# A decoder layer on one core: sums over keys and gate product in column groups of TensorE, with normalisations moved from VectorE to ScalarE and GpSimd

## The reference

```python
x = layernorm(x + attention(x))          # rotary q and k, attention between the heads of one token
x = layernorm(x + xattn(x, ctx, ctx))    # an mLSTM cell: q = x, k = v = ctx
x = layernorm(x + ffn(x))                # 8 low-rank experts, one chosen for each token

def xattn(q, k, v):                      # for each head, s and t over 128 tokens
    ig, fg = concat(q, k, v) @ Wi + bi, concat(q, k, v) @ Wf + bf
    F = cumsum(log_sigmoid(fg))
    log_D = tril(F[s] - F[t] + ig[t])
    C = (q @ k.T) / sqrt(32) * exp(log_D - rowmax(log_D))
    n = maximum(abs(C.sum(-1)), exp(-rowmax(log_D)))
    h = (C / (n + 1e-6)) @ v             # the "sums over keys"
    return headwise_layernorm(h) * ln_scale
```

## Time and profile before

| | us |
|---|---|
| three runs | 1919.57, 1921.3, 1925.41 |
| median | 1921.3 |
| span of the profiled execution, first to last instruction | 1919.0 |
| busy: PE, DVE, ACT, POOL | 1766.6, 1557.8, 783.8, 759.3 |

### The profile page before, as it was taken

One profiled execution on the slowest core, in us unless ns is written; L12 is line 12 of the kernel. 1 busy time (PEld: TensorE's weight loads), 2 busy tenths in 40 slices (PEclk: granted clock), 3 DMA queues, 4 the chain that ended last, 5 costly groups with the idle time before them and its releaser, 6 DMA issues.

```text
span 1919.0 us, 67339 instructions
## 1 busy us (share of the span) xinstructions
PE 1766.6 (92%) x27529; PEld 1464.6 (76%) x27656; DVE 1557.8 (81%) x3898; ACT 783.8 (41%) x2193; POOL 759.3 (40%) x779
## 2 busy tenths in 40 slices
PE   0889999999999999999999999999999999999985
PEld 0678787887887788788778778878877877887863
DVE  4456888888888888888888888888888888888876
ACT  2134344434434434443443444444344344444431
POOL 1034344334434433433443443343344344334333
PEclk9999999999999999999999999999999999999985
DMA  4112222221221222222122222222212222222110
GB/s 138 60 58 75 70 67 84 78 82 60 82 77 66 80 75 67 79 81 78 63 80 77 66 82 73 69 77 82 77 66 77 77 66 82 74 76 69 66 57 28
DMA packets 53829, 141.14 MB, mean 74 GB/s; under 512 B 8767, under 2 KB 10431, under 8 KB 45578
## 3 DMA queue, kind: packets, MB, share of 16 engines
q1 hardware_dynamic: 53770, 140.31, 21.4%
HBM read 122.98 MB, written 17.30 MB: 73 GB/s over the span
## 4 chain that ended last, share of the span: by engine, by line
PE 83%; DVE 6%; ACT 6%; issue 3%; SPq 1%; POOL 0%; DMA 0%; POOLq 0%; ACTq 0%; DVEq 0%
PE bank L493 12%; PE bank L365 10%; PE bank L366 9%; PE bank L368 9%; PE bank L347 8%; PE bank L355 4%; PE quad L481 4%; PE bank L448 4%; PE bank L460 3%; PE bank L507 3%; PE bank L360 3%; PE bank L356 3%; PE bank L519 3%; PE bank L462 3%; ACT x_high L584 2%
## 5 line engine op out<-in xcount | busy, mean ns | idle before, releaser
L734 POOL TENSOR_TENSOR ex<-ex,w_rec 128x512 f32<-128x512 f32 x64 | 67.2, 1050 | 766.4 <-DVE w_rec L848 766.4
L642 ACT ACTIVATE Dx<-Mb,a_col 128x128 f32<-128x128 f32 x1024 | 313.0, 397 | 0.0
L493 PEld LDWEIGHTS bank<-c,Dx 128*128 128x128 f32 x2048 | 244.4, 192 | 30.1 <-ACT LT L672 21.6
L493 PE MATMUL bank<-c,Dx 128*128 128x33 f32 x2048 | 246.7, 276 | 17.1 <-ACT LT L672 14.7
L746 POOL TENSOR_TENSOR h_rs<-h_ve,half_neg 128x16 f32<-128x16 f32 x64 | 186.9, 2921 | 147.1 <-DVE h_ve L934 147.1
L615 ACT ACTIVATE x1T<-bank 128x512 f32<-128x512 f32 x64 | 38.3, 598 | 357.8 <-PE bank L347 357.8
L913 DVE SCALAR_TENSOR_TENSOR Dx<-quad,Dx 128x512 f32<-128x512 f32 x256 | 159.0, 683 | 11.5 <-PE quad L481 2.8
L760 POOL TENSOR_TENSOR rs<-ve,half_neg 128x1 f32<-128x1 f32 x192 | 106.1, 553 | 155.0 <-DVE ve L869 154.9
L739 POOL TENSOR_SCALAR_AFFINE_SELECT Dx<-Dx 128x512 f32<-128x512 f32 x256 | 159.8, 637 | 5.4 <-ACT Dx L642 5.4
L594 ACT ACTIVATE ex<-ex 128x512 f32<-128x512 f32 x64 | 40.3, 630 | 239.3 <-DVE ex L839 239.3
L347 PE MATMUL bank<-id_sb,x 128*128 128x128 f32 x512 | 85.7, 291 | 54.9 <-DVE x2sq L954 53.0
(11 more groups left out here) (157 smaller groups left out, 4351.5 us busy)
## 6 DMA issues: line engine op xcount, KB each, us to landing
Mb<-m_rows SPq DMA_DIRECT2D x64, 1024.0 KB, 4.6
xb<-in_x SPq DMA_DIRECT2D x256, 64.0 KB
xr<-in_x SPq DMA_DIRECT2D x64, 256.0 KB, 2.6
cb<-in_ctx SPq DMA_DIRECT2D x64, 256.0 KB, 3.5
out_dram<-yo SPq DMA_DIRECT2D x64, 256.0 KB, 2.4
Dx<-in_wq SPq DMA_DIRECT2D x4, 256.0 KB, 4.5
Dx<-in_wk SPq DMA_DIRECT2D x4, 256.0 KB, 5.5
Mb<-in_wv SPq DMA_DIRECT2D x4, 256.0 KB, 5.6
```

What stands on the lines that cost most here:

```text
L493: last = mm(bank[6 + h // 8][:, (h % 8) * HD:(h % 8 + 1) * HD], Dx[t.parity()][:, h % 4, h // 4, :], c1[:, h, :], start=True, stop=True)
L642: last = go(Dx[t.parity()][:, j, n, :], Mb[t.parity()][:, h, :], ACT.Exp, bias=a_col[t.parity()][:, h:h + 1], scale=-1.0)
```

## The change

Names are those of the functions in the listing; the lags and the parity buffers are as before unless told.

- **Sums over keys**: `heads` is replaced by `m_HT`, in which `c1` (128x32) is the stationary operand and `Dx` streams its 128 columns, four heads at a time in the four column groups of the array, and by `m_H`, which turns the result `HT` back with four matmuls of 132 columns against a constant `back`. `back` also subtracts each head's mean and extracts the row sum. `m_HT` stands behind `a_S`, `m_H` behind `m_cT`, and ScalarE copies `HT` in between.
- **Centering**: `m_c1` on PE and its copy on ScalarE go; GpSimd subtracts the head's first column from the context instead, so that the first column of `c1` can hold the one.
- **Gate product**: `m_part` has 32 stationary columns for each 128 rows, in four column groups; ScalarE copies the four partial sums (`g4`), and one matmul against `pick` adds them up (`m_gate`).
- **Gate functions**: |x| and max(-x, 0) on ScalarE; `log_f` and `g_abs` go from DVE, and the scan takes both its inputs at once.
- **Normalisations**: epsilon, power and minus mean times scale on GpSimd, subtract and scale in one ScalarE instruction (`a_x1`, `r_x2`, `x_yo`). `r_y` goes to GpSimd as well.
- **Order**: on PE `m_QK` stays behind `p_k`, `m_x1T` goes behind `x_LT`, `a_S` in front of the gate product, and `x_x2T` behind `p_q`. On DVE k is turned (`p_KT`) right behind the statistics of the first normalisation, and `m_scan` moves from the end of a step to behind `a_rec` of the next. `x_shift` and `r_stats` open the step. The store is one step later (LAGS 7).

```diff
+            def m_part(t):
+                pe.wait_ge(s.x1T_sb, upto(t))
+                edge(pe, t, (s.cT_sb, 0))
+                for n in range(CH):
+                    mm(bank[5][32 * n:32 * n + 32, 0:P], wg_x1[:, n, :], x1T[t.parity()][:, n, :], start=True, stop=False,
+                       tile_position=(0, 32 * n))
+                for n in range(CH):
+                    last = mm(bank[5][32 * n:32 * n + 32, 0:P], wg_ctx[:, n, :], cT[t.parity()][:, n, :], start=False,
+                              stop=True, tile_position=(0, 32 * n))
+                last.then_inc(s.part_ps, 1)
+
             def m_gate(t):
...
+                pe.wait_ge(s.g4_sb, upto(t))
+                mm(bank[5][0:GW, P:2 * P], pick[:], g4[:], start=True, stop=True).then_inc(s.gate_ps, 1)
...
             def m_QK(t):
-                for j in range(3):
-                    pe.wait_ge(s.Dm_sb[j], upto(t))
...
+            def m_HT(t):
+                pe.wait_ge(s.LT_sb, upto(t, 3))
+                pe.wait_ge(s.c1_sb, upto(t))
+                edge(pe, t, (s.Hs_sb, 1), (s.acol_sb, 0), *[(s.C_sb[j], 0) for j in range(4)])
+                for n in range(CH):
+                    for j in range(4):
+                        last = mm(bank[7][32 * j:32 * j + 32, n * P:(n + 1) * P], c1[t.parity()][:, 4 * n + j, :],
+                                  Dx[t.parity()][:, j, n, :], start=True, stop=True, tile_position=(0, 32 * j))
+                last.then_inc(s.HT_ps, 1)
...
-            def heads(t, lo, hi):
-                for h in range(lo, hi):
-                    last = mm(bank[6 + h // 8][:, (h % 8) * HD:(h % 8 + 1) * HD], Dx[t.parity()][:, h % 4, h // 4, :],
-                              c1[:, h, :], start=True, stop=True)
-                return last
+                pe.wait_ge(s.HT_sb, upto(t))
+                edge(pe, t, (s.KT_sb, -2))
+                for n in range(CH):
+                    last = mm(bank[6 + n // 2][:, (n % 2) * 4 * HD:(n % 2 + 1) * 4 * HD], HT[:, n * P:(n + 1) * P],
+                              back[:].rearrange("p h d -> p (h d)"), start=True, stop=True)
+                last.then_inc(s.H_ps, 1)
...
+            def a_x1(t):
+                act.wait_ge(s.nm1_sb, upto(t))
+                edge(act, t, (s.r2_sb, 2), (s.x1T_ps, 2))
+                go(x1[t.parity()][:], r1[:], ACT.Identity, bias=nm1[:], scale=rs1[:]).then_inc(s.x1_sb, 1)
...
+            def m_c1(t):
+                pool.wait_ge(s.c_in[t.parity()], landed(t, 1))
+                pool.wait_ge(s.HT_ps, upto(t, 2))
+                heads = cb[t.parity()][:].rearrange("p (h d) -> p h d", d=D)
+                tt(c1[t.parity()][:, :, 1:D], heads[:, :, 1:D], heads[:, :, 0:1].broadcast_to([P, H, D - 1]),
+                   ALU.subtract).then_inc(s.c1_sb, 1)
...
+            def r_y(t):
+                pool.wait_ge(s.hrs_sb, upto(t))
+                pool.wait_ge(s.x2_sb, upto(t, 1))
+                pool.wait_ge(s.acol_sb, upto(t, -1))
+                tt(r2[:].rearrange("p (h d) -> p h d", d=D), Hs[:, :, 0:D],
+                   h_rs[:].unsqueeze(2).broadcast_to([P, H, D]), ALU.mult).then_inc(s.y1_sb, 1)
                 pool.wait_ge(s.y1_sb, upto(t))
                 tt(r2[:], r2[:], lns_sb[:], ALU.mult).then_inc(s.y2_sb, 1)
...
+            def rsqrt(t, mv, ve, rs, nm, mv_sem, ve_sem, rs_sem, nm_sem, used):
+                pool.wait_ge(mv_sem, upto(t))
+                edge(pool, t, (used, 1))
+                tt(ve[:], mv[:, 1:2], eps[:], ALU.add).then_inc(ve_sem, 1)
                 pool.wait_ge(ve_sem, upto(t))
...
                 tt(rs[:], ve[:], half_neg[:, 0:1], ALU.pow).then_inc(rs_sem, 1)
+                pool.wait_ge(s.pads_set, PADS)
+                pool.wait_ge(rs_sem, upto(t))
+                ts(nm[:], mv[:, 0:1], rs[:], -1.0, ALU.mult, ALU.mult).then_inc(nm_sem, 1)
...
             def m_scan(t):
                 dve.wait_ge(s.gln_sb, upto(t))
...
                 edge(dve, t, (s.aT_ps, 1))
-                tt(a_row[:], gs[0:H, :], Fs[:], ALU.subtract).then_inc(s.a_sb, 1)
+                nc.vector.tensor_tensor_scan(Gs[:], g_relu[32:GW, :], g_ln[32:GW, :], 0.0, ALU.add,
+                                             ALU.add).then_inc(s.G_sb, 1)
+                dve.wait_ge(s.G_sb, upto(t))
+                tt(a_row[:], gs[:], Gs[:], ALU.add).then_inc(s.a_sb, 1)
```

More of the change, by code:

```diff
@@ L45 @@
 ML_EPS = 1e-6
-LAGS = 6
-PADS = 7
+LAGS = 7
+PADS = 15
+MATS = 25
 PEEL = 10
@@ L422, in a_O @@
                 pe.wait_ge(s.VG_sb, upto(t))
-                edge(pe, t, (s.sub_sb, 0), *[(s.C_sb[j], 2) for j in range(4)])
+                edge(pe, t, *[(s.C_sb[j], 2) for j in range(4)])
                 for v in range(4):
@@ L528, in _ @@
             pe.wait_ge(s.bias_step, 15)
-            pe.wait_ge(s.center_set, 11)
+            pe.wait_ge(s.mats_set, MATS)
             def step(a):
                 b, c, d, e, f, g = [a.older(n) for n in range(1, 7)]
+                if b.real():
+                    a_S(b)
+                if c.real():
+                    m_part(c)
+                if d.real():
+                    m_HT(d)
                 if c.real():
@@ L567, in step @@
                     m_QK(c)
-                if b.real():
-                    m_x1T(b)
                 if e.real():
@@ L573, in step @@
                     x_LT(f)
+                if b.real():
+                    m_x1T(b)
             steps(pe, step)
@@ L685, in step @@
             def step(a):
-                b, c, d, e, f = [a.older(n) for n in range(1, 6)]
+                b, c, d, e, f, g, h = [a.older(n) for n in range(1, 8)]
+                if c.real():
+                    m_x1T(c)
+                if g.real():
+                    x_LT(g)
+                if h.real():
+                    x_yo(h)
+                if c.real():
+                    m_g4(c)
+                if b.real():
+                    a_exp(b)
                 if d.real():
-                    r_sq(d)
+                    m_HT(d)
+                if c.real():
+                    m_softplus(c)
                 if f.real():
@@ L698, in step @@
                     p_xT(a)
+                if d.real():
+                    r_sq(d)
+                if c.real():
+                    m_acol(c)
                 if b.real():
                     a_O(b)
+                if e.real():
+                    r_x2(e)
                 if c.real():
-                    m_c1(c)
                     m_Dx(c, 2)
-                    m_Dx(c, 0)
-                    m_Dx(c, 1)
                 if e.real():
@@ L762, in _ @@
             pool.wait_ge(s.const_in, CONST_IN)
             nc.gpsimd.memset(half_neg[:], -0.5).then_inc(s.pads_set, 1)
-            nc.gpsimd.memset(c1[:], 1.0).then_inc(s.pads_set, 1)
-            tt(wg_ctx[:], wg_sb[:, 1], wg_sb[:, 2], ALU.add).then_inc(s.pads_set, 1)
+            nc.gpsimd.memset(eps[:], LN_EPS).then_inc(s.pads_set, 1)
+            for i in range(2):
+                nc.gpsimd.memset(c1[i][:], 1.0).then_inc(s.pads_set, 1)
+            part = wg_sb[:].rearrange("p m c (a n) -> p m c a n", n=H)[:, :, :, 0:3:2, :]
@@ L766, in _ @@
+            for c in range(CH):
+                tt(wg_ctx[:, c].rearrange("p (a n) -> p a n", n=H), part[:, 1, c], part[:, 2, c],
+                   ALU.add).then_inc(s.pads_set, 1)
+                nc.gpsimd.tensor_copy(wg_x1[:, c].rearrange("p (a n) -> p a n", n=H), part[:, 0, c]).then_inc(s.pads_set, 1)
+            ts(bg_neg[:], bg_sb[:], -1.0, 1.0, ALU.mult, ALU.mult).then_inc(s.pads_set, 1)
             pool.wait_ge(s.pads_set, PADS)
@@ new lines, in _ @@
+            dve.wait_ge(s.mats_set, 16)
+            nc.vector.tensor_copy(pick[:].rearrange("p (a n) -> p a n", n=H)[:, 0:3:2, :],
+                                  pick2[:].rearrange("p (a n) -> p a n", n=H)).then_inc(s.mats_set, 1)
+            for i in range(4):
+                nc.vector.memset(back[32 * i:32 * i + 1, :, :], 0.0).then_inc(s.mats_set, 1)
+            dve.wait_ge(s.mats_set, 21)
+            for i in range(4):
+                nc.vector.memset(back[32 * i:32 * i + 1, i, D:HD], 1.0).then_inc(s.mats_set, 1)
```

372 lines of the change are left out of this document (151 added, 221 removed).

## The result

The change makes the kernel slower: 2139.2 us, median of four runs (2126 to 2147), against 1923.4 for the kernel before; the ratio is 1.111, 95% interval 1.107 to 1.116. The forecast was 1766 us. The profiled execution took 2126.1 us with a span of 2124.4.

The account below looks back on a forecast made before the run. The prediction took PE, 92% busy, to bound the kernel, with DVE not far behind. Cutting 60 steps from 28.19 to 25.6 us saves 155 us: 1919.0 to 1764 us of span, 1766 us measured; range 1690 to 1865.

Parts of the forecast that it names:

- The period. Two engines in turn limit the step, PE at 24.7 and DVE at 25.6: Step period after the change: the longer of PE's and DVE's periods, 25.6 us, where it was 28.19.
- the edits costed at nothing: ScalarE's and GpSimd's added work, the first scaling's chain, later `M_row`, SyncE's context load, and LAGS 7's drain: set to zero.
- the four rivals: Column groups take turns (chance 0.12), GpSimd's passes take over (0.09), weight loads in the open (0.09), no change (0.02).
- both meet at the scores, so the longer one holds: PE and DVE join at the scores, so the step is the longer period, 25.6 us.
- GpSimd's passes take over: DVE instructions beside GpSimd passes lose up to 4.9 us a step: 27.2 us, 1862 us; chance 0.09.
- its signs: For GpSimd's passes: line 1014 and the scan's difference far above 0.3 us, PE waiting for DVE's turn of v.
- the middle of the forecast: DVE's step: 19.08 us of work plus 1.6 to 4.9 us lost beside GpSimd's passes.
- Removed and added PE work: PE: 6.37 us a step removed, 1.65 (48 column-group records) and 1.18 (ten ordinary matmuls) added; work 23.60 us.
- the groups don't take turns: Rival on PE: column groups take turns, 0.118 us a record, 48 cost 5.66 us; 1951 us, slower; chance 0.12.
- the loads aren't in the open: Rival from the skill's rule that loads overlap only across row groups: 48 records 2.58 us, 1820 us; chance 0.09.
- The new wait: On PE before the scores, for DVE's four `m_C`: 2.48 plus 0.2 hand-overs, less 1.62 covered, 1.06 us.
- The direction: Faster 0.86 (forecast, GpSimd and weight loads), same 0.02, slower 0.12 (column groups taking turns).

Follow-up runs that it names:

- the run with 139: Kernel after (its loop in place) with 139 idle instructions (waits on a long-set semaphore) ahead of TensorE's loop: 1868.9 us, ratio 0.972 to the kernel before.
- the run with v turned first: Kernel after with 139 idle instructions, GpSimd's `m_c1` held back, v turned ahead of VectorE's gate chain, expert output product ahead of gate-row transposes: 1719.9 us, ratio 0.894.
- the runs with 85 and 149 idle instructions: Kernel after with 85 or 149 waits-only instructions ahead of TensorE's loop: 2153.6 us with 85, 1891.7 us with 149.

## Why the prediction was wrong

**The step that failed: "The period. Two engines in turn limit the step, PE at 24.7 and DVE at 25.6".** A third thing limits it, the delivery of PE's instructions. The sum priced work and semaphore waits and had no term for fetching, not even among the edits costed at nothing; none of the four rivals had one either. The runs show its size: 270 us, the time between the same work with its loop fetched again and held. The kernel before gave no wait to see, since its loop was held; what there was to read was the queue's row of 42 packets, the length of the loop, and that edits to the written-out steps move where it begins. Of the 4.85 us a step between after and the same kernel with the loop in place (32.16 - 27.31), 2.55 are more idle time and 2.30 more busy time (418.64 of 500 us busy at a clock of 0.88 are 26.93 us of a step; 450.88 are 24.63); around the stalls shown above, from 1001.80 to 1005.70, the granted clock is 0.50, and from 1008.30 to 1012.00 it is 1.00. How much of the 2.30 is the stalls' doing the runs don't tell beyond that.

**A second step failed: "both meet at the scores, so the longer one holds".** In place, the change takes 1868.9 us where the forecast said 1766: a step of 27.31 instead of 25.6. The two engines meet twice in a step, at the scores and at the turned v, and PE's work and its waits add up: 24.63 + 1.55 for `VT` (74.4 / 48) + 1.14 for `m_C` (53.5 / 47) = 27.32 us. The forecast had the second wait (1.06) and not the first, and it had PE's work at the full clock (23.60).

27.31 is close to the upper bound of the rival *GpSimd's passes take over* (27.2 us, 1862), and its signs are there: PE waits for DVE's turn of v, and the scan's difference `a_row` takes 840 ns. The passes do hold DVE up: the new `m_c1` costs `a_row` 840 - 279 = 561 ns, and through the wait it costs PE clock as well. But the rival's sum is not what happened, and that its time fits is chance: DVE is busy 22.17 us a step (405.81 of 500), the middle of the forecast (19.08 + 3.25 = 22.33) and not its bound (24.0). What was missed is where the lost time lies: v's turn stands behind the whole gate chain in DVE's queue, and PE waits for it.

**Removed and added PE work was right.** With the loop in place, 48 column-group records take 1.45 us (1020.84 to 1022.29 in the run with 139), forecast 1.65, 0.030 each:

```profile
1020.84 0.43 PE L452 MATMUL bank<-x1T,wg_x 128*32 128x128 f32 x8
1021.09 0.40 PE L455 MATMUL bank<-cT,wg_ctx 128*32 128x128 f32 x8
1021.30 1.06 PE L485 MATMUL bank<-Dx,c 128*32 128x128 f32 x32
1022.29 0.42 PE L461 MATMUL bank<-g,pick 128*48 128x128 f32 x2
```

So the groups don't take turns (0.118), and the loads aren't in the open (0.054): the rule of the Trainium skill's "TensorE: Matmul & The Clock Gate", Part 3, that the prediction weighed is not borne out for these records. The after trace alone would have misled: there `m_HT` takes 1.77 us, 0.055 a record, at a granted clock of 0.58 (1006.56 to 1008.30), against 1.00 here. PE's work of a step was forecast as 23.60 us; it is 476.72 / 500 x 24.62 = 23.47 in the run with v turned first, where the clock is 1.00.

**The new wait was right.** PE waits 1.14 us for `m_C` with the loop in place, forecast 1.06; the 0.2 us for hand-overs in that forecast come from no row.

**The direction.** "Slower" had its chance by the column groups alone, which is not what happened; the range ended at 1865 because every case in it was made of work and semaphores. With the loop in place the change is faster, as forecast, but 1868.9 still lies just outside that range.

## What to carry to other kernels

Before pricing an edit to a kernel with a long loop, count the loop's instructions on each engine and where it begins: a loop of 6.9 packets on TensorE was held where it lay within seven packets (25 of 256 places, by the boundaries above); where it stuck out by 32 instructions or more, the place cost 157 to 386 us, by kernel, whatever the edit was worth. Compare the instruction queue's packets with the length of the program: here far more packets than length, with waits at issue inside the loop, meant a loop that is fetched again. Idle instructions ahead of it (139 here), put where the engine waits anyway, mended it, and the edit could then be judged by itself.

## What the runs showed of the hardware

- A shift of TensorE's program by 32 idle instructions (from 7878 to 7846) took the time from 1878.6 to 2153.6 us; one that leaves the loop's end 8 instructions behind the seven packets brought 72 packets more, where a fetch at each of the 26 jumps brings 234.
- The issue stalls inside the loops that are fetched again fall at instruction 7880 and multiples of 256 from it, within one instruction, in the kernel after and in the runs with 85 and 149 idle instructions.
- Small VectorE instructions that begin beside a GpSimd pass of 1.0 to 1.1 us end with it: 840 ns against 279 for `a_row`, 1007 against 412 for the scan.
- A wait of 1.56 us on PE went with a granted clock of 0.94 over the stretch (0.69 in the 5 us behind the wait), one of 0.9 us (and 1.14 at another place, in both) with 1.00.
